# Attention with relative positions and a routed expert layer: each step's third score part issued ahead of its value pass, expert weights loaded early, key rows filled and values stored in the first stage

## The reference

```python
q, k, v = proj(Wq, bq), proj(Wk, bk), proj(Wv, bv)        # 16 heads of width 16
idx = clip(r[None, :] - r[:, None], -128, 128) + 128      # distance of key and query
scores = (q @ k.T + einsum('bhqd,qkd->bhqk', q, rel_k[idx])) / 4
w = softmax(scores)
s = (w @ v + einsum('bhqk,qkd->bhqd', w, rel_v[idx])) @ Wo.T + bo
expert = argmax(xn @ Wg + bg)                              # one of 8
g = silu(gelu(xn @ W1[expert]) @ W2[expert])
out = x + s * g
```

## Time and profile before

| | us |
|---|---|
| median of 3 runs (lowest, highest) | 2410.63 (2409.11, 2410.94) |
| profiled execution, its own time | 2410.91 |
| its span, first to last instruction | 2409.2 |
| PE busy | 2303.6 (96%) |
| ACT busy | 1767.1 (73%) |
| DVE busy | 1694.8 (70%) |
| POOL busy | 1356.6 (56%) |

### The profile page before, as it was taken

The page is one execution under the profiler, slowest core; times in us unless marked ns, Lnnn a source line. Parts: engine busy times, 40 slices in busy tenths (PEclk is TensorE's granted clock), DMA queues, the critical chain, the costliest instruction groups (busy, mean ns, idle before and its releaser), DMA issues. The chain is left out here.

```text
span 2409.2 us, 46760 instructions
## 1 busy us (share of the span) xinstructions
PE 2303.6 (96%) x14320; PEld 1159.1 (48%) x14320; DVE 1694.8 (70%) x4408; ACT 1767.1 (73%) x4108; POOL 1356.6 (56%) x3283
## 2 busy tenths in 40 slices
PE   7839999999999999999999999999999998899998
PEld 4403444444444444444444444444444444667676
DVE  7678777777777777777777777777777761333333
ACT  5515888888888888888888888888888886221211
POOL 2326666666666666666666666666666666433332
PEclk9957999999999999999999999999999999999999
DMA  6667898788888888878888788878888762922221
GB/s 198 197 196 248 278 294 272 246 258 254 262 257 252 259 254 263 259 247 257 256 259 253 248 258 254 261 244 254 257 258 258 238 202 101 315 64 69 64 68 49
DMA packets 349605, 541.04 MB, mean 225 GB/s; under 512 B 29088, under 2 KB 257808, under 8 KB 349360
## 3 DMA queue, kind: packets, MB, share of 16 engines
q1 hardware_dynamic: 331904, 502.72, 66.4%
q0 software_dynamic: 17456, 35.33, 4.9%
HBM read 272.60 MB, written 269.43 MB: 225 GB/s over the span
## 5 line engine op out<-in xcount | busy, mean ns | idle before, releaser
L1148 DVE TENSOR_REDUCE part<-ps 128x1 f32<-128x512 f32 (+3 forms) x2048 | 1166.2, 589 | 371.8 <-PE ps L976 353.6
L1198 ACT ACTIVATE probs_T<-pst 128x256 f32<-128x256 f32 (+2 forms) x2012 | 1033.3, 528 | 175.2 <-PE pst L990 170.6
L976 PE MATMUL ps<-k_front,q_front 96*128 96x512 bf16 x2048 | 803.3, 392 | 25.8 <-DVE part L1146 20.4
L924 PE MATMUL pout<-probs_T,v_far 128*32 128x512 f32 (+3 forms) x4864 | 546.0, 535 | 7.7 <-ACT probs_T L1198 5.5
L976 PEld LDWEIGHTS ps<-k_front,q_front 96*128 96x128 bf16 x2048 | 197.2, 96 | 441.2 <-DVE part L1148 239.0
L990 PE MATMUL pst<-q_back,k_right 102*128 102x512 bf16 (+1 forms) x1012 | 344.3, 342 | 0.2 <-ACT probs_T L1198 0.2
L990 PE MATMUL pst<-q_back,k_left 102*128 102x256 bf16 (+1 forms) x1000 | 342.6, 343 | 0.0
L814 POOL TENSOR_TENSOR left<-left 128x256 f32<-128x256 f32 (+5 forms) x768 | 280.5, 365 | 60.2
L1211 ACT ACTIVATE band<-band,negm 128x384 f32<-128x384 f32 (+1 forms) x512 | 309.7, 605 | 0.0
L1146 DVE CUSTOM_DVE_ANT_0 band<-ps,band 128x256 f32<-128x256 f32 (+2 forms) x704 | 299.4, 425 | 0.0
L924 PEld LDWEIGHTS pout<-probs_T,v_far 128*32 128x32 f32 x4864 | 163.6, 108 | 248.8 <-issue 196.8
(11 more groups left out here) (168 smaller groups left out, 2426.4 us busy)
## 6 DMA issues: line engine op xcount, KB each, us to landing
rel_scores<-rel SPq DMA_DIRECT2D x128, 1024.0 KB, 8.5
band_probs<-band SPq DMA_DIRECT2D x128, 768.0 KB, 4.0
pwin<-band_probs SPq DMA_DIRECT2D x128, 512.0 KB, 6.3
band<-rel_scores SPq DMA_DIRECT2D x64, 768.0 KB, 6.7
band<-rel_scores SPq DMA_DIRECT2D x64, 576.0 KB, 5.4
w<-in_w_dram SPq DMA_DIRECT2D x16, 1024.0 KB, 15.8
band<-rel_scores SPq DMA_DIRECT2D x64, 128.0 KB, 5.8
q_terms<-terms SPq DMA_DIRECT2D x48, 128.0 KB
```

Of the source, the lines that this page charges most:

```text
L924: return nc.tensor.matmul(pout[32 * g:32 * g + 32, c0:c1], values, probs, start=first, stop=False, skip_group_check=True)
L976: nc.tensor.matmul(ps1[u % 2][:, :], q_front[a.par][:, a.s * P:(a.s + 1) * P], k_front[a.par][:, u * CW:(u + 1) * CW], start=True, stop=Tr ...
L1148: ins = nc.vector.tensor_reduce(peak, src, AX_X, ALU.max)
L1198: ins = nc.scalar.activation(probs_T[t.s % 2][:, u * CW + c0:u * CW + c1], score_bank(a, u)[:, c0:c1], ACT.Exp, scale=SCALE)
```

## The change

In PE's loop the score part `u + 1` is issued before the value pass instead of after it; the value pass keeps its place after key-major part `u`. So part 2 moves ahead of it in most steps, part 3 where a pair's values begin. There are three further edits: `k_left` and `k_right` are now filled by GpSimd in `project`; the wait for the values' stores moves from the end of `project` to the first reader of the values on SP and to the first write of `attn` on DVE; and `w1` is allocated for the whole kernel, its room being lent to `project`'s tiles and to `band`, `rel`, `pwin` and `pwin_T`, and five of its eight loads (experts 0 to 4) are issued in the drain of the last pair, when their room has come free. `attn`'s room holds the values in `project`.

```diff
@@ project, GpSimd
+                pool.wait_ge(ident_set, 4)
+                for p in range(2):
+                    pool.memset(con["k_left"][p][ROWS:ALLROWS, :], 0.0).then_inc(shift_set, 1)
+                    pool.memset(con["k_right"][p][ROWS:ALLROWS, :], 1.0).then_inc(shift_set, 1)
...
-                pool.wait_ge(v_out, 16 * B)
@@ attend, SyncE
                             wait(sp, v_built, x.count(1, 0))
+                            if x.n == 0:
+                                sp.wait_ge(v_out, 16 * B)
...
+                    if at_end(hb) and off == 2 * NB + 4:
+
+                        sp.wait_ge(bandT_mm, 16 * (NBH - 1))
+                        sp.wait_ge(left_ready, 4 * (NBH - 1))
+                        for r in range(4):
+                            sp.wait_ge(prob_out[r], 16 * (NBH - 1))
+                        load_experts(0, EARLY)
+                        for r in range(4):
+                            sp.wait_ge(rel_out[r], 16 * NBH)
+                        load_experts(EARLY, LATER)
...
+                def load_experts(first, last):
+                    for e in range(first, last):
+                        sp.dma_start(w1[:, e], io["w1"][e].rearrange("(c p) f -> p c f", p=P)).then_inc(w1_in, 16)
@@ attend, TensorE
+                    def scores(u):
+                        if a.s == 0 and u == 0:
+                            pe.wait_ge(qf_in[a.par], a.count2(48, 48))
+                            pe.wait_ge(kf_in[a.par], a.count2(48, 48))
+                        wait(pe, s1_used, a.count(64, 4 * a.s + u - 1))
+                        nc.tensor.matmul(ps1[u % 2][:, :], q_front[a.par][:, a.s * P:(a.s + 1) * P], k_front[a.par][:, u * CW:(u + 1) * CW],
+                                         start=True, stop=True).then_inc(s1_mm, 1)
+
+                    values_at = 2 if w.s == 0 else 1
                     for u in range(CH):
-                        if a.valid:
...
+                        if a.valid and not (w.valid and u == values_at + 1):
+                            scores(u)
...
-                        if u == (2 if w.s == 0 else 1) and w.valid:
+                        if u == values_at and w.valid:
+                            if a.valid:
+                                scores(u + 1)
                             key_values()
@@ attend, VectorE
-                for p in range(2):
-                    nc.vector.memset(k_left[p][ROWS:ALLROWS, :], 0.0).then_inc(shift_set, 1)
-                    nc.vector.memset(k_right[p][ROWS:ALLROWS, :], 1.0).then_inc(shift_set, 1)
...
@@ experts, SyncE
-                for e in range(NE):
+                for e in range(NB * BAND // (DC * FF) + 2, NE):
                     sp.dma_start(w1[:, e], io["w1"][e].rearrange("(c p) f -> p c f", p=P)).then_inc(w1_in, 16)
```

More of the change, by code:

```diff
@@ L103, in sem, with lent @@
             return ctx.enter_context(nc.semaphore(name))
-        x_all = sb("x_all", [P, TILES, D], F32)
+        taken = [0]
+        def lent(*dims):
+            n = 1
+            for d in dims:
+                n *= d
+            room = w1[:, :, :, :].rearrange("p e c f -> p (e c f)")[:, taken[0]:taken[0] + n]
+            taken[0] += n
+            return room.rearrange("p (a b) -> p a b", b=dims[1]) if len(dims) == 2 else room
+        x_all = lent(TILES, D)
         wq = sb("wq", [P, DC, D], F32)
@@ L137, in project @@
         ident_set = sem("ident_set")
+        shift_set = sem("shift_set")
         stats_done = sem("stats_done")
@@ L222, in _ @@
                                        pattern=[[-1, P]], channel_multiplier=1).then_inc(ident_set, 1)
+                pool.wait_ge(ident_set, 4)
+                for p in range(2):
+                    pool.memset(con["k_left"][p][ROWS:ALLROWS, :], 0.0).then_inc(shift_set, 1)
+                    pool.memset(con["k_right"][p][ROWS:ALLROWS, :], 1.0).then_inc(shift_set, 1)
+                pool.wait_ge(shift_set, 4)
+                for p in range(2):
+                    pool.memset(con["k_left"][p][ROWS:ROWS + SHIFTS // 2, :], 1.0).then_inc(shift_set, 1)
+                    pool.memset(con["k_right"][p][ROWS:ROWS + SHIFTS // 2, :], 0.0).then_inc(shift_set, 1)
+                pool.wait_ge(shift_set, 8)
                 v_pairs = dram["v"].rearrange("(h b) p i d -> b p h (i d)", b=B)
@@ L460, in attend @@
         q_back = two("q_back", [ALLROWS, S], BF16)
[L461 to L466, removed]
+        k_left, k_right = con["k_left"], con["k_right"]
+        EARLY = NB * BAND // (DC * FF)
+        LATER = EARLY + 2
+        band = [w1[:, 0:EARLY].rearrange("p e c f -> p (e c f)").rearrange("p (i w) -> p i w", w=BAND), sb("band1", [P, NB, BAND], F32)]
+        rel = [w1[:, EARLY + i].rearrange("p c f -> p (c f)").rearrange("p (i w) -> p i w", w=WIN) for i in range(2)]
+        pwin = [w1[:, LATER, i].rearrange("p (r w) -> p r w", w=NEARW) for i in range(2)]
+        pwin_T = w1[:, LATER + 1:NE].rearrange("p e c f -> p e (c f)")
         left = sb("left", [P, CH, P], F32)
@@ L1214, in _, with experts @@
                 loop(step)
-def experts(nc, io, dram, con, attn, expert_i, slots_filled, slots, wo, bo, out):
+def experts(nc, io, dram, con, attn, expert_i, slots_filled, slots, w1, w1_in, wo, bo, out):
     SG, SR = 2, 4
@@ L1524, in build @@
             lg_all = early.enter_context(nc.sbuf_tensor("lg_all", [P, TILES, NE], F32))
-            project(nc, io, dram, con, lg_all)
-            attend(nc, io, dram, con, lg_all, pos_i, expert_i, slots_filled, wo, bo, attn)
-        experts(nc, io, dram, con, attn, expert_i, slots_filled, slots, wo, bo, out)
+            for name in ("k_left", "k_right"):
+                con[name] = [early.enter_context(nc.sbuf_tensor(f"{name}{i}", [ALLROWS, S], BF16)) for i in range(2)]
+            project(nc, io, dram, con, lg_all, w1, attn, v_out)
+            attend(nc, io, dram, con, lg_all, pos_i, expert_i, slots_filled, w1, w1_in, wo, bo, attn, v_out)
+        experts(nc, io, dram, con, attn, expert_i, slots_filled, slots, w1, w1_in, wo, bo, out)
 _INS = ["x", "wqT", "wkT", "wvT", "wg", "bq", "bk", "bv", "bg", "rel_kT", "rel_v", "woT", "bo", "w1", "w2"]
```

32 lines of the change are left out of this document (11 added, 21 removed).

## The result

The changed kernel takes 2566.99 us (median of 4 runs, 2565.69 to 2569.61), the kernel before beside it 2410.26 (4 runs, 2409.11 to 2410.94): ratio 1.0652, 95% interval 1.0638 to 1.0665. It is slower by 157 us; 2552 was forecast, with a range of 2510 to 2580.

A forecast was written before the change was run, and what follows sets the result against it. PE's queue was taken to bound the loop, with DVE waiting for PE. 2410.9 + 153 (main edit) - 10.3 (values' store and key rows) - 1.5 (expert weights) = 2552 us, range 2510 to 2580.

The forecast's parts named there:

- S2: Attention loop on PE: third score part of a step; overwrites the first part's PSUM bank, so waits until DVE reduced that.
- steps 0 to 15: Loop steps of a batch-head, numbered by query block; claimed costs 0.16 to 0.69 us each, sum 5.19 us a round.
- given back ... 7 us: Loop: step 3's value pass no longer waiting, about 0.05 us, and key-major part following the pass directly, about 0.01 a step.
- The values' store: End of first stage: without the wait for the second values' store, the loop stage starts earlier; 4.5 us gained (3 to 5).
- The key rows: Opening: fills moved from DVE to idle GpSimd cost nothing there and let the routing's counts come earlier; 5.8 us gained.
- Expert weights: Drain of the last head: five early first-layer loads shorten output projection bubble and second-layer weight wait; -1.5 us (-7 to +16).
- Rival (4): Drain of the last head: early weight loads hold up the last windows; +16, 2568 us; chance 5%.
- (1): Loop: DVE was the brake and the early third score part removes its 0.56 us idle; faster, 2389 us; chance 4%.
- (2): Loop: waits exist but only the bare chain counts, without short DVE jobs ahead; +115, 2514 us; chance 8%.
- (3): Loop: PE's clock falls to half for a tenth of it; +150, 2700 us; chance 3%.
- PE's idle time before score parts near 150 us: Sign in the profile after: total PE idle ahead of score parts, released by DVE, would be near 150 us.
- The first parts at about 151: Sign in the profile after: the loop's first score parts would come at about 151 us in place of 161.27.

## Why the prediction was right, and where it was not

**The bound and the mechanism: right.** PE's queue was the bound, S2 waits in it for DVE, and nothing behind it goes first. With the order alone: 161 us.

**The size of a step: right to some hundredths.** Measured by the distance of first parts, the steps 0 to 15 lost 0.24, 0.19, 0.49, 0.71, 0.39, 0.27, 0.46, 0.35, 0.45, 0.30, 0.38, 0.19, 0.19, 0.10, 0.36 and 0.17 us; sum 5.23 against 5.19. Times 30.8 rounds it is 161. What was wrong is the "given back ... 7 us" behind it: T2 directly behind the value pass gives nothing (1295.93 less 1294.93 is the 1.00 us that S2 had to wait before), and step 3's own 0.05 did not come back either. Without that correction the term would have been 160, against 161.5 measured.

**The values' store: wrong, -4.5 became -1.1 to -1.5 at the seam, and nothing in the medians.** The step that failed is "Without that wait the last landing is the key terms'". The wait in the program was not the only thing that held the block's end. The trace of before could have warned: GpSimd's DRAIN there, from 129.34, took 2.19 us after everything had landed, and no row told what it costs with a store in flight. No gain at all should have been one of the bounds, and was not.

**The key rows: half right.** -5.8 was -6.5 where it was looked for. The step that failed is "so the fills cost nothing there". GpSimd was idle, but its fills held DVE's TENSOR_SCALARs, and DVE was the engine that the stage waited for. That is +4.3 us by the transposes of the third chunk. Another +2.1 came in between 88 and 101 us, where ACT waits 1.32 us for DVE and 0.8 us longer than before for the query terms' landing; why is open. With the last value matmul at 119.88 instead of 113.47, the opening's sum is +6.4 (first stage) - 1.5 (seam) - 6.5 (counts) = -1.6, as measured. This is one execution: in the three others with the fills on GpSimd the first stage was 3.8 to 5.4 us longer than before, and step 18 came 2.8 to 3.2 us earlier.

**Expert weights: right.** -1.2 against -1.5 for all that comes after the last score part. The loads did go out early and held nothing up: from the last score part to the projection's first transpose it is 58.2 us in both kernels. SP's row (start, time of issue, count), then PE's:

```profile
2145.19 2.96 SPq L770 DMA_DIRECT2D w<-in_w_dram  x5
```

```profile
2215.11 0.69 PE L1382 MATMUL pt<-ident,at 128*128 128x128 f32 x2 [5.25 <-DVE at L1484]
```

The bubble of the earlier trace rows went from 6.35 to 5.25 us and the wait of 0.79 us for second-layer weights is gone. From the projection's first transpose to the first expert tile the four profiled kernels with early loads take 45.4 to 46.4 us, and the eight without 48.0 to 48.6, so the gain there is some 2 to 3 us. In the changed kernel the expert tiles took 0.9 us more, which brings the sum to -1.2; that it fell so near to -1.5 is partly luck. Rival (4) did not occur.

**The other rivals.** (1) did not: DVE's idle time moved and grew. (2) would have needed 115 us; the short DVE jobs ahead of S0 count fully, as step 2 with 0.49 us and step 3 with 0.71 show. (3): the clock stayed at 1.00 from 280 to 1966 us, though PE paused in the steps of 3.9 us for 0.10 to 0.71 us.

**What was to be seen.** The mean step grew by 0.327 us (0.31 said), S2 follows DVE's end by 0.06, DVE's waits grew. "PE's idle time before score parts near 150 us" was wrong as put: the page shows 105.5, of which 25.8 were there before, since the modelled ends hide the rest. "The first parts at about 151" was wrong too: 159.70.

## What to carry to other kernels

An instruction moved ahead in an in-order queue brings its wait with it. Before moving it, take the end of what it waits for and the time at which the queue gets there; where a long instruction between the two covers the wait, the move costs the difference in every step. Idle time of an engine that is not the bound, like DVE's here, is no reason for such a move. A wait taken out at a block's end should be checked against what the engine itself waits for there, and an engine that looks idle is free only if what it touches is: GpSimd's fills held VectorE's small operations.

## What the runs showed of the hardware

**The price of a narrow matmul alone.** The Trainium skill's page "TensorEngine Tiling (Array Packing)", section "Key Properties", says that a change of tiling mode drains the array; with the pass cut in two, the second entry cost 0.10 us, like the first (0.09). A gap at each entry fits that; no run shows that it is the drain. The dear part was another: one 32-column matmul that has no other column groups beside it takes 0.77 us (384 columns).

**One stage that differs between chips.** With the old order the loop's mean step is 3.580 us on all chips used, within 0.001, but the drain of the pipeline, from the last score part to the first product of the output projection, takes 59.1 to 59.4 us on the chip of the first comparison and on that of the divided pass and the stores, and 82 to 86 us on the others (the program's order there is the same). That is nearly all of the 25 us between 2410 and 2435. Windows over it, with the fills on DVE (kernel before at 2435 us), and with the store moved as well (kernel before at 2411 us):

```profile
1973.00:2054.00 81.00, 55.58 (x379) 25.59 (x376) 4.59 (x13) 48.31 (x109) 42.13 (x65) 0.89 0.13 40
```

```profile
1972.00:2031.00 59.00, 49.91 (x381) 23.33 (x378) 5.22 (x15) 47.38 (x111) 42.44 (x66) 1.00 0.19 56
```

The same work, with 16 us more idle time on PE, 6 us more busy time and a granted clock of 0.89 in place of 1.00. The waits of the first of the two in that stretch (total, times, longest):

```profile
PEld pout L930 <- ACT probs_T L1196: 22.2, 15, 4.7
POOL slots L1314 <- POOLq L664: 18.7, 1, 18.7
PE pout L930 <- ACT probs_T L1196: 15.2, 13, 4.4
PEld pout L930 <- issue: 14.0, 20, 7.6
ACT probs_T L1196 <- remote: 11.4, 7, 3.8
```

Waits with "issue" and "remote" as the releaser, up to 7.6 us long, stand there where the other chip has no "remote" and at most 0.8 us of "issue" at a time. What holds the engines back in those moments stays open. It is a reason to compare kernels only within one chip.
